# Attention with post-norm and routed low-rank experts: the opening and first batch laid anew, P V blocks by twos

## The reference, cut to what matters

```
def attention(x, wq, wk, wv, wo):
    xq, xk, xv = x @ wq.T, x @ wk.T, x @ wv.T          # 16 heads of 32
    scores = einsum('bqhd,bkhd->bhqk', xq, xk)         # not scaled
    probs = softmax(scores, axis=-1)
    return einsum('bhqk,bkhd->bqhd', probs, xv) @ wo.T

def experts(x, A, B, Wr, br):                          # 8 experts of rank 64
    probs = softmax(x @ Wr.T + br); pick = argmax(probs)
    y = (x @ A[pick].T) @ B[pick].T / 64
    return y * max(probs)

x = layernorm(x + attention(x)); x = layernorm(x + experts(x))
```

## Time and profile before

| | us |
|---|---|
| median of three runs | 1601.32 |
| the profiled execution | 1602.13 |
| its span | 1600.2 |
| TensorE busy | 1520.6 |
| GpSimd busy | 1184.0 |
| VectorE busy | 999.9 |
| ScalarE busy | 772.8 |

### The profile page before, as it was taken

How to read it: one execution, slowest core, us unless ns; L and a number is a source line. 1 busy time by engine, 2 the same in 40 slices (tenths; PEclk the granted TensorE clock), 3 DMA queues, 4 the chain that set the end, 5 groups by cost and what they waited for, 6 DMA issues and landing times.

```text
span 1600.2 us, 20249 instructions
## 1 busy us (share of the span) xinstructions
PE 1520.6 (95%) x6816; PEld 836.2 (52%) x6816; DVE 999.9 (62%) x1764; ACT 772.8 (48%) x1421; POOL 1184.0 (74%) x655
## 2 busy tenths in 40 slices
PE   6798979999999999999999999999999999999898
PEld 5664436666545555555644554555654444453354
DVE  5575576665586766656568667665556776672433
ACT  3154545555455454455545454544554545555222
POOL 0087889899977768777788876678877888889601
PEclk9898989999999999999999999999999999999999
DMA  7933334545232332237342133333433222210001
GB/s 230 295 99 97 99 105 139 153 140 142 84 99 64 83 93 76 71 100 221 96 146 47 58 89 87 83 110 104 171 90 100 48 47 58 57 41 21 7 1 53
DMA packets 79287, 156.27 MB, mean 98 GB/s; under 512 B 19008, under 2 KB 25168, under 8 KB 78800
## 3 DMA queue, kind: packets, MB, share of 16 engines
q1 hardware_dynamic: 77520, 152.33, 33.4%
q0 software_dynamic: 608, 2.12, 0.4%
q10 hardware_dynamic: 1056, 0.52, 0.1%
HBM read 105.66 MB, written 48.49 MB: 96 GB/s over the span
## 4 chain that ended last, share of the span: by engine, by line
PE 79%; DVE 8%; DMA 4%; issue 3%; SPq 2%; POOL 2%; ACT 1%; ACTq 0%; POOLq 0%; DVEq 0%
PE w L566 16%; PE sc L684 14%; PE pv L696 13%; PE mx L674 13%; PE w L643 5%; PE w L630 5%; PE w L601 5%; DVE mxc L885 3%; PE mx L655 2%; DMA stack<-qk_parts 2%; DVE xT_s L902 1%; PE w L623 1%; DVE gate L995 1%; DVE eq L990 1%; SPq L344 1%
## 5 line engine op out<-in xcount | busy, mean ns | idle before, releaser
L885 DVE TENSOR_REDUCE mxc<-mx 128x1 f32<-128x512 f32 x1024 | 680.7, 685 | 449.2 <-PE mx L674 447.5
L770 ACT ACTIVATE P<-sc 128x512 f32<-128x512 f32 x1024 | 594.6, 596 | 607.7 <-PE sc L684 592.5
L501 POOL TENSOR_TENSOR Psum<-Psum,P 128x1024 f32<-128x1024 f32 x300 | 711.0, 2396 | 45.7 <-ACT P L770 42.3
L684 PE MATMUL sc<-stack 98*128 98x512 f32 x1024 | 547.2, 536 | 7.7 <-ACT P L770 3.8
L674 PE MATMUL mx<-stack 96*128 96x512 f32 x1024 | 409.4, 403 | 26.5 <-DMA stack<-qk_parts 15.9
L684 PEld LDWEIGHTS sc<-stack 98*128 98x128 f32 x1024 | 195.3, 191 | 202.1 <-ACT P L770 94.8
L696 PE MATMUL pv<-P,V 128*32 128x512 f32 x2048 | 274.4, 608 | 0.0
L674 PEld LDWEIGHTS mx<-stack 96*128 96x128 f32 x1024 | 197.5, 193 | 130.8 <-issue 57.4
L566 PE MATMUL w<-xT_s,wqk_s 128*128 128x512 f32 x768 | 227.6, 411 | 20.8 <-DVE xT_s L902 13.2
L498 POOL TENSOR_TENSOR Psum<-P 128x1024 f32<-128x1024 f32 x50 | 117.8, 2376 | 147.8 <-PE mx L655 113.8
L566 PEld LDWEIGHTS w<-xT_s,wqk_s 128*128 128x128 f32 x768 | 144.2, 194 | 93.2 <-issue 55.2
(11 more groups left out here) (125 smaller groups left out, 1017.6 us busy)
## 6 DMA issues: line engine op xcount, KB each, us to landing
stack<-qk_parts SPq DMA_DIRECT2D x192, 256.0 KB, 5.5
qk_parts<-split SPq DMA_DIRECT2D x64, 512.0 KB, 3.2
wqk_s<-wqk_parts SPq DMA_DIRECT2D x30, 512.0 KB, 4.9
xT_s_f<-xT SPq DMA_DIRECT2D x8, 1024.0 KB, 11.2
den_s<-den_parts SPq DMA_DIRECT2D x124, 64.0 KB, 2.0
r<-x SPq DMA_DIRECT2D x3, 2048.0 KB, 9.4
out<-r SPq DMA_DIRECT2D x12, 512.0 KB, 3.9
wide<-wv_parts SPq DMA_DIRECT2D x2, 2048.0 KB, 12.0
```

Source lines behind the costliest of these rows:

```text
L501: pool.tensor_tensor(sums(s)[:, i, :], sums(s)[:, i, :], P[:, unit % NP, :], ALU.add).then_inc(add_done, 1)
L684: pe.matmul(sc[c][:, :], stack(s, i)[0:KS, 0, 128 * kb:128 * kb + 128], stack(s, i)[0:KS, 1, 512 * c:512 * c + 512], start=True, stop=True ...
L770: act.activation(P[:, unit % NP, 512 * c:512 * c + 512], sc[c][:, :], ACT.Exp).then_inc(exp_done, 1)
L885: dve.tensor_reduce(mxc[:, q % 2, m:m + 1], mx[TURN[g] % NMX][:, :], AX.X, ALU.max).then_inc(mx_done, 1)
```

## The change

- **Loads.** x's second half is issued when the first has landed (also for later batches, at halves 3 and 9 of their slot, each after that half's score). wv's load waits for the second half. Raw slices come in three groups. wo is loaded in slot 7.
- **Opening.** Four `qk` pieces, in an order that needs x's second half only for the third; `v` 0 to 5, `max_t`, `v` 6 and 7. The first pair's operands are loaded by halves: the first after two `qk` pieces are stored. The 32 `mx` tiles stand in `v` 1 to 5, those that need only the first half at the front.
- **Weights.** Batch 0's projections read the split slices where they were made (`attT`, `r`); the slices are stored to DRAM one at each 8th half of slots 0 and 1, and come back in slot 2 for batch 1.
- **Fill.** Slots 0 to 2 have 4 `qk` pieces (slot 0 within its first 24 halves), slot 3 two from half 18, slot 4 five, slots 5 and 6 four, slot 7 one and four `v`. Float32r passes are laid singly instead of by three.
- **Maxima.** Slot 0 does 32 items and not 40, slot 1 does 44.
- **Stacks.** At half 0, head 1 of slot s+1, first in SP's order; at half 14 (slot 0: 28), after that half's score, head 0 of slot s+2.
- **Sums.** In slots 0 to 3 and 31, GpSimd leaves the last two units out, 12 adds and not 14; `den` adds those two P buffers itself, a second group of 4 matmuls. `den` then comes at half 6. Second sums of batch 0 lie in `wo_s`, not in `r`.
- **P V.** In slots 0 to 7 and in the first, second and last slots of each later batch, blocks are issued two at a time at every fourth unit.

```
-    PLAN[at], PLAN[at + 1], PLAN[at + 2] = qks(0, 7, 3), qks(0, 10, 3), qks(0, 13, 3)
-    PLAN[at + 3], FROM[at + 3] = qks(1, 0, 1), 25
     for n in range(3):
-        PLAN[at + 4 + n] = qks(1, 1 + 5 * n, 5)
-    PLAN[at + 7] = tiles("v", 1, 0, 4)
+        PLAN[at + n] = qks(0, 4 + 4 * n, 4)
+    TO[at] = 24
+    PLAN[at + 3], FROM[at + 3] = qks(1, 0, 2), 18
+    PLAN[at + 4], PLAN[at + 5], PLAN[at + 6] = qks(1, 2, 5), qks(1, 7, 4), qks(1, 11, 4)
+    PLAN[at + 7] = qks(1, 15, 1) + tiles("v", 1, 0, 4)
...
-OPENING = qks(0, 0, 4) + tiles("v", 0, 0, 8) + qks(0, 4, 1) + [("max_t", 0)] + qks(0, 5, 2)
+OPENING = qks(0, 0, 4) + tiles("v", 0, 0, 6) + [("max_t", 0)] + tiles("v", 0, 6, 2)
+EARLY = {("v", n, PASSES * kt + PASSES - 1): 1 + (n > 2) for n in range(1, 6) for kt in range(KT)}
...
+    if s < 2:
+        late = 3 * s
+        until = MAXES * (s + 1) + min(MAXES, max(0, MAXES * (h + 1 - late) // (MAX_AT - late)))
+        if s and h >= MAX_AT:
+            until += 2 * (h + 1 - MAX_AT)
+    else:
+        until = half + 1 + MAXES + 2 * LEAD
...
+def tail(s):
+    return s < 4 or s == LAST
+def adds(s):
+    return UNITS - 2 - 2 * tail(s)
+def blocks(s, k):
+    if s >= PAIRS and 2 <= s % PAIRS < PAIRS - 1:
+        return ((k - 3) // 2,) if k % 2 and k >= 3 else ()
+    return ((k - 5) // 2, (k - 3) // 2) if k % 4 == 1 and k >= 5 else ()
...
         def load_weights(j):                                        # SP
+            sp.wait_ge(slices_stored, 32 * SLICES)
+            sp.wait_ge(qk_ready, 4 if j < SLICES + 2 else 2 * (j - 1))
+        def load_first(c):
+            for stored in qk_stored:
+                sp.wait_ge(stored, 16 * (c + 1))
+            for i in range(2):
+                load_parts(0, i, slice(512 * c, 512 * c + 512), (loaded0[0], loaded1[0])[i] if c else first_half[i])
...
         load_x(0, 0)
         load_x(0, 1)
-        sp.wait_ge(x_loaded[0], 16)
-        load_raw(slice(128, D))
-        for n in range(4):
-            store_qk(n)
-        for q in range(2):
-            for i in range(2):
-                load_stack(q, i)
-        for j in range(SLICES):
-            store_slice(j)
...
+        load_raw(1, slice(128, 256))
+        store_qk(0)
+        store_qk(1)
+        load_first(0)
+        store_qk(2)
+        store_qk(3)
+        load_first(1)
+        for i in range(2):
+            load_stack(1, i)
+        load_raw(2, slice(256, D))
         load_max(0)
...
-            if h == (0 if s else 14) and s + 2 < SLOTS:
+            if h == (14 if s else 28) and s + 2 < SLOTS:
+                sp.wait_ge(sc_ready, half)
                 load_stack(s + 2, 0)
...
+                if b == 0 and p % 2 == 0 and p:                     # GpSimd, normalise
+                    pool.wait_ge(slices_stored, 32 * SLICES)
+                    pool.wait_ge(qk_ready, 2 * p + 4)
...
-            for n, (i, j) in enumerate(((0, 0), (0, 1), (1, 0))):   # TensorE
-                done = pe.matmul(bank[:, :], weights[i], moving[j], ...)
+            i, j = ((0, 0), (0, 1), (1, 0))[c % PASSES]
+            return pe.matmul(bank[:, :], weights[i], moving[j], start=(c == 0), stop=(c == PASSES * KT - 1))
...
-            if c == 1 and k == 1 and s:
-                out_block(s - 1, KB - 1)
-            if c == 1 and k % 2 == 1 and k >= 3:
-                out_block(s, (k - 3) // 2)
+            if c == 1 and s:
+                for kb in blocks(s - 1, UNITS + k):
+                    if kb < KB:
+                        out_block(s - 1, kb)
+            if c == 1:
+                for kb in blocks(s, k):
+                    out_block(s, kb)
...
         slice_high(0)                                               # ScalarE
+        for m in range(KT): x_high(0, m)
+        slice_high(1)
+        for m in range(KT, KT + 2): x_high(0, m)
+        hi_part(0)
+        for m in range(KT + 2, 2 * KT): x_high(0, m)
+        hi_part(1)
+        for kt in range(KT): wv_high(kt)
+        hi_part(2)
+        hi_part(3)
+        for n in range(2):
+            slice_high(2 + n)
+            copy_v(n)
+        for n in range(2, 6):
+            copy_v(n)
+            slice_high(2 + n)
```

More of the change, by code:

```diff
@@ L120, in build_attention_lora_moe_block @@
         chunks = [(kind, n, c) for kind, n in PLAN[s] for c in range(CHUNKS[kind])]
-        begin, spent, total = FROM.get(s, 0), 0, sum(cost(kind) for kind, _, _ in chunks)
+        begin, end, spent, total = FROM.get(s, 0), TO.get(s, HALVES), 0, sum(cost(kind) for kind, _, _ in chunks)
         for kind, n, c in chunks:
-            half = HALVES * s + begin + int((HALVES - begin) * (spent + cost(kind) / 2) / total)
+            half = HALVES * s + begin + int((end - begin) * (spent + cost(kind) / 2) / total)
             AT.setdefault(half, []).append((kind, n, c))
@@ L132, in build_attention_lora_moe_block @@
     for half in range(HALVES * SLOTS):
-        until = half + 1 + MAX_AHEAD if half >= HALVES else MAXES + (half + 1) * MAX_AHEAD // HALVES
-        ITEMS[half] = range(made, min(until, MAXES * SLOTS))
-        made = max(made, min(until, MAXES * SLOTS))
+        s, h = divmod(half, HALVES)
+        if s < 2:
[5 more added lines that the diff above has]
+            until = half + 1 + MAXES + 2 * LEAD
+        ITEMS[half] = range(made, max(made, min(until, MAXES * SLOTS)))
+        made = ITEMS[half].stop
     def second(s):
         return s % 2 == 1 and (s < PAIRS - 1 or s > PAIRS * (B - 1))
-    def den_at(s):
-        return 10 if second(s) != second(s - 1) or s % PAIRS == 2 else 6
+    def tail(s):
+        return s < 4 or s == LAST
+    def adds(s):
+        return UNITS - 2 - 2 * tail(s)
+    ADDS_BEFORE = [sum(adds(q) for q in range(s)) for s in range(SLOTS + 1)]
+    def den_at(s):
+        return 10 if not tail(s - 1) and (second(s) != second(s - 1) or s % PAIRS == 2) else 6
+    def blocks(s, k):
+        if s >= PAIRS and 2 <= s % PAIRS < PAIRS - 1:
+            return ((k - 3) // 2,) if k % 2 and k >= 3 else ()
+        return ((k - 5) // 2, (k - 3) // 2) if k % 4 == 1 and k >= 5 else ()
     TURN, turn = {}, 0
@@ L378, in load_stack @@
                     sp.wait_ge(sc_ready, HALVES * (free + 1))
[L379 to L382 removed]
+                load_parts(q, i, slice(0, S), (loaded0[q % 3], loaded1[q % 2])[i])
             def load_max(q):
@@ L456, in _ @@
                     load_wv(b + 1)
+                if h == 2 and s == PAIRS - 1:
+                    load_wo()
                 if h == 16 and p == 7 and b < B - 1:
@@ L545, in _ @@
                         normalise(s - back, added, deviations)
-                if h % 2 and h >= 4:
+                if h % 2 and 2 <= h // 2 < adds(s) + 2:
                     add(s, h // 2)
@@ L588, in v @@
                         pe.wait_ge(wv_loaded, 16 * (b - 1))
-                if n == 0:
+                if n == 0 and c % PASSES == 0:
                     pe.wait_ge(wv_lo, kt + 1)
-                done = three(bank, [xT_s[:, i, kt, 128 * kb:128 * kb + 128] for i in range(2)], [wide[:, i, kt, :] for i in range(2)], kt)
-                if kt == KT - 1:
+                done = one_of_three(bank, [xT_s[:, i, kt, 128 * kb:128 * kb + 128] for i in range(2)],
+                                    [wide[:, i, kt, :] for i in range(2)], c)
+                if c == PASSES * KT - 1:
                     done.then_inc(v_ready, 1)
@@ L650, in den @@
                     pe.wait_ge(mx_done, TURN["den", s] - NMX + 1)
-                pe.wait_ge(add_done, ADDS * (s + 1))
-                for c in range(2):
-                    for i in range(2):
-                        at = HD * (2 * c + i)
-                        done = pe.matmul(bank[at:at + HD, :], ones[:, :], sums(s)[:, i, 512 * c:512 * c + 512],
-                                         start=True, stop=True)
+                pe.wait_ge(add_done, ADDS_BEFORE[s + 1])
+                for n in range(1 + tail(s)):
+                    for c in range(2):
+                        for i in range(2):
+                            at = HD * (2 * c + i)
+                            block = P[:, (UNITS * (s + 1) - 2 + i) % NP, :] if n else sums(s)[:, i, :]
+                            done = pe.matmul(bank[at:at + HD, :], ones[:, :], block[:, 512 * c:512 * c + 512],
+                                             start=(n == 0), stop=(n == tail(s)))
                 done.then_inc(den_done, 1)
@@ L729, in _ @@
                     KIND[kind](n, chunk, bank)
-            out_block(LAST, KB - 1)
+            for kb in blocks(LAST, UNITS + 1):
+                out_block(LAST, kb)
             pe.wait_ge(exp_done, 2 * UNITS * SLOTS)
@@ L1036, in _ @@
                     max_item(g)
+                if s == 0 and h in (2, 4, 6, 8):
+                    slice_low(3 + h // 2)
                 if h == MAX_AT and s < LAST:
```

230 lines of the change are left out of this document (119 added, 111 removed).

## The result

| | before | after |
|---|---|---|
| median | 1601.78 (1600.3 to 1609.59, 7 runs) | 1584.57 (1583.66 to 1593.72, 7 runs) |
| span of the profiled execution | 1600.2 | 1582.8 |
| granted clock, mean | 0.982 | 0.984 |

The ratio is 0.9902, interval 0.9885 to 0.992: faster by 1.0%, or 17 us, where 47 was forecast. 1584.57 lies outside the range of 1543 to 1580. The direction was right, the size was not.

What follows compares the result with a forecast made beforehand. The prediction took TensorE's work, plus the stretches in which it has none, to bound the kernel. From 1602.13 us it took 36.5 for batch 0 and 11.0 for later slots and the end, giving 1555, range 1543 to 1580.

Steps and rivals of the forecast that it cites:

- Slot 0, 36.5: Batch 0's first slot: 32.5 us of passes and pairs without a denominator, plus 4 for slow clock and unfilled last halves.
- Slot 3, 38: Batch 0's fourth slot: 38 us, as reordered stack loads and x by halves end a 7.1 us stall.
- Its second stretch stays: Later part of slot 3: VectorE still filled for 23.2 of 24.7 us by reductions and splits of x.
- Opening, 56: Everything before slot 0: first score at 56 us instead of 75.75.
- Slots 1, 2, 4, 5, 6: These slots of batch 0 were forecast at 42.5, 37.8, 39.5, 36.2 and 36.2 us.
- The price of a pair: Two P V blocks issued together save 0.29 us, within 0.20 to 0.35, where TensorE is the bound.
- Rival B: Inside a pair, the second block's weights wait for the first to end: 6 us more, 1561; chance 0.15.
- Pairs in the later slots: Paired blocks save 6.9 us in slots 8, 16, 24, 25, 15, 23, 1.1 in 9 and 17, 0.5 in 31.
- End, 2.5: Last denominator: two fewer GpSimd adds clear a 3.37 us wait, an extra group costs 0.9; saving 2.5 us.
- The single passes: nothing, +-2: Float32r passes laid singly are the same matmuls with the same loads: no effect, bounds +-2 us.
- A: Rival: transfers still set slots 0 to 3, through stalls and lost clock: +20 us, 1575; chance 0.20.
- D: Rival: pairs starve the exponentials and TensorE waits 1.2 us per pair: 82 us more, 1637; chance 0.04.

Runs made afterwards that it cites:

- e1: The changed kernel with the low parts of weight slices 4 to 7 made before slot 0 instead of at its halves 2 to 8: 1576.91 us, ratio 0.9826.
- e3: The changed kernel with the second projection of batch 1 moved from slot 3 to slot 4: 1582.86 us, ratio 0.987.
- e2: The changed kernel with the last raw weight slices loaded before the first pair's first halves, not behind the second pair's operands: 1583.79 us, ratio 0.9871.
- e9: The changed kernel with float32r passes of projections and V laid by three again instead of singly: 1584.72 us, ratio 0.9869.
- e11: The changed kernel with all 14 adds of slot 31 on GpSimd and one group in its denominator, as before: 1591.19 us, ratio 0.9916.

## Why the prediction was wrong, step by step

- **Slot 0, 36.5: the step that failed first and cost most.** Its sum had TensorE, the denominator and the clock, and nothing for "slices 4 to 7 get theirs at halves 2, 4, 6 and 8 of slot 0". I had the price of such subtractions beside GpSimd in the earlier trace rows (1.5 us each for a 0.68 one) and applied it to slot 3 alone. Bounded by that row, four would have been 3.3 us of VectorE; measured, one alone was 7.74 and cost TensorE 7.14 and the clock behind it (e1: 9.4 of the slot, 9.8 of the span). The Trainium skill, SBUF — State Buffer, Who interferes with whom, says that a VectorE instruction with two SBUF inputs contends with a GpSimd instruction that reads SBUF. It calls the shared ports an exclusive lock and, of VectorE's two-port modes, says that the one that issues first holds them for the whole of its instruction. The ends 0.55 after an add agree with that; 7.74 over three adds, with the subtraction started 0.22 ahead of the first, is more than it says.
- **Slot 3, 38: failed.** The stacks' stall went, as predicted. "Its second stretch stays" was the fault: 23.2 us of VectorE work was there before too, but with one projection from half 25 behind it. The change puts two from half 18 on, so TensorE meets x's low parts; my sum had the stacks alone as what is late there. I didn't set the parts' times against the projections'. e3, with one, measured 38.68.
- **Opening, 56: half failed.** First matmul 10.32 (10.4), the load by halves and the weights in place came as priced. The four projections did not: "48 passes, to 21.7" takes every pass at 0.234, and they ended at 24.1, with the first thirteen at 0.43, 2.4 late. I named the chain raw slices, split of slice 4, `copy_v` of V 3, V 5, and gave it 1 us (0 to 3) without a row; it cost 4.25 of waiting, and the clock behind it: e2 gives 5.1. The two make 7.5, less the 1 us that I had given: most of the 7.1.
- **Slots 1, 2, 4, 5, 6: right** within 0.5, but slot 2 was 1.8 better: the waits I couldn't place weren't there. Slot 1 is partly luck: TensorE was busy 41.24 where my sum had 39.5, and waited 1.4 and not 3 (0.8 of it for a stack). Slots 5 and 6 took the 35.8 that TensorE's own sum gave, and GpSimd's floor of 36.1 wasn't their bound: in slot 5 TensorE is busy 35.73 of 35.75 and GpSimd 32.25. GpSimd came late one slot on: slot 7, 1.1 longer than forecast, has one wait, 1.2 for GpSimd's sum.
- **The price of a pair: right**, 0.32 for 0.29 in a range of 0.20 to 0.35, and a second group starts 0.89 after the first, not 0.99. Rival B fell: the loads of a second group stand in the trace while the first group's matmuls run. The rule that I had put behind it is one of two: the same page of the Trainium skill, TensorE: Matmul & The Clock Gate, says under Step-by-step: what each phase is for, that a load also goes ahead of running matmuls where it targets the background weight buffer. The 0.89 agrees with that.
- **Pairs in the later slots: sign wrong in four.** Where TensorE was the bound they gave 1.4 (slots 8, 16, 24, 25), and 2.2 in 15 and 23, where one block fewer comes over from the lone slot in front (1.19 + 3 x 0.32): 10.0 for the forecast 6.9. The same hand-over costs slots 10 and 18 0.87 each, which I didn't see (slot 26 has it too and kept 43.05); their other 1.4 came with the single passes (e9). Slots 9 and 17 were priced at half a gain, and came out 2.4 and 2.6 longer, which the runs explain in part only. Slot 31, priced at a gain of 0.5, is 0.8 longer, with 6.8 us at the lower clock and not 3.4; slot 27's 2.3 was in no term.
- **End, 2.5: right**: 4.5 in the two profiles, some 3 over all of them (e11).
- **"The single passes: nothing, +-2": right** in sum (e9), though several slots move.
- **Rivals.** A gave 1575 for transfers. Only the late raw slices of the opening were that, 5 of the 25 us; the waits for stacks are 0.8 us. Its size was nearest, mostly by luck. D, exponentials starved behind pairs, didn't come: the wait of scores for ScalarE in the first 250 us is 1.6 us in all, five times. None of the rivals had a stall on VectorE.
